# ScalarE's rounds in an experts' loop: eight pairs long in place of four, each pair's expert word loaded within the steps

## The chip, the cores and the metric

The kernel runs on one core of a Trainium2 chip. The metric is the device time of one execution, in microseconds (us); lower is better. Engines are named as the profile names them: PE is TensorE (PEld its weight loads), DVE is VectorE, ACT is ScalarE, POOL is GpSimd, SP is SyncE.

## The reference, cut to what matters

The input x has 4 batches of 1024 tokens of width 256. It is normalised, and the output is x plus an attention plus a mixture of experts, both of the normalised x. The part that the change touches is the mixture:

```python
def body(acc, ws):
    wg, wu, wdn, cw = ws
    hmid = jax.nn.silu(x @ wg) * (x @ wu)
    return (acc + cw[:, None] * (hmid @ wdn), None)
y, _ = jax.lax.scan(body, jnp.zeros_like(x), (We_gate, We_up, We_down, w_dense.T))
```

There are 64 experts of 256 x 128 (gate and up) and 128 x 256 (down), and every token picks 8 of them, so that the weight `cw` of most token and expert pairs is zero.

## The kernel before, in words

**The stages.** First the input is normalised, the router's scores are made and the slots of all token copies are worked out. Then attention is done for the first 18 of 32 blocks of 128 tokens, while GpSimd scatters copies of the tokens into a table in HBM in which each tile of 128 rows belongs to one expert. Then comes the experts' loop, and then the attention of the last 14 blocks, beside which the experts' results are added up. In the profiled execution the experts' loop fills about us 616 to 1218 of the span.

**The experts' loop.** There are 320 tiles, taken two at a time: 160 pairs (`PAIRS`). The tiles of a pair may belong to different experts. No scheduler is at work: each engine has its own instruction stream, written out by hand, and the streams meet at semaphores. For pair u they do this:

- ScalarE's queue loads the pair's rows, four pairs ahead (`load_pair`, L1265), into one of four buffers (`XS` = 4, shown as pr and qz).
- TensorE turns the pair's tiles into PSUM (`turn_tiles`, L966, 4 transposes), two pairs ahead; ScalarE copies them back (`keep_tiles`, L1243, sm<-psT).
- ScalarE copies the gate and up weights of the pair's two experts out of a ring of eight experts (`keep_weights`, L1261, two copies wt<-shared_mem), two pairs ahead, into one of two buffers. It has to know which experts: one word for each pair, e1 * 64 + e0, lies in `pair_row`, and `experts_of` (L1253) loads it into a register and takes the two numbers out of it.
- TensorE multiplies by gate and up (`gate_up`, L982, shown as 16 matmuls), one pair ahead; ScalarE applies Silu (`silu`, L1249, prT<-psS), VectorE multiplies the halves (`make_h`, L1683), TensorE multiplies by down (`down`, L991, shown as 4 matmuls), VectorE copies the result (`keep_y`, L1690), and GpSimd scatters it to HBM (L669).

TensorE's order in the step of pair u is `turn_tiles(u+2)`, `down(u-1)`, `gate_up(u+1)`. It may start `down(u)` when `make_h(u)` is done, and `gate_up(u+2)` when the weights and the turned tiles of pair u+2 are there. ScalarE's order in the step of pair u is `silu(u)`, `keep_tiles(u+2)`, `keep_weights(u+2)`, `load_pair(u+4)`.

**The rounds.** The loops are hardware loops over rounds of unrolled steps. TensorE's rounds are eight pairs long (`PE_ROUND`), and it loads each pair's word in the step before. VectorE's and GpSimd's are four long. ScalarE's are four long as well: 1 unrolled round of four, 38 in a hardware loop (L1288), 1 unrolled at the end, and at the head of each it loads the words of all four pairs whose weights it will copy. VectorE's rounds 1 to 32 hold extra work (`slot_weights`, L1494) for each pair.

Of the kernel before, what the change touches and what calls it, by code (L numbers as in the profile page):

```python
# [38 lines left out]
PAIRS = TILES // 2  # L39
MID_TILE = TILES // 2  # L40
assert MID_TILE <= 256
PE_ROUND = 8
XS, YS = 4, 4
ROW = 272
META = K + 1
# [12 lines left out]
MANY = 9  # L58
# [12 lines left out]
def build(nc, A, out):  # L71
    with ExitStack() as ctx:
# [6 lines left out]
        def sem(name):  # L79
            return ctx.enter_context(nc.semaphore(name))  # L80
# [254 lines left out]
        row_meta = sem("row_meta")  # L335
# [347 lines left out]
        def _(pe):  # L683
# [276 lines left out]
            def turn_tiles(j, u, turn, first):  # L960
                pe.wait_ge(xs_in[j], 16 * (turn + 1))
                if not first:
                    pe.wait_ge(xsT_ready, u - 1)
                for a in range(2):
                    for c in range(DC):
                        last = nc.tensor.transpose(psT[:, j % 2, (a * DC + c) * P:(a * DC + c + 1) * P],  # L966
                                                   xs[j][:, a, c * P:(c + 1) * P], ident[:])
                last.then_inc(xs_turned, 1)

            def experts_of(u):  # L970
                word = pe.value_load(pair_row[0:1, bass.ds(u, 1)], min_val=0, max_val=E * E - 1)
                return word % E, word // E
# [13 lines left out]
            def down(j, u, experts, first):  # L986
                pe.wait_ge(h_ready, u + 1)
                if not first:
                    pe.wait_ge(y_kept, u - 1)
                for a, e in enumerate(experts):  # L990
                    last = mm((psM, psO)[j % 2][:, a * D:(a + 1) * D], hT[:, j % 2, a, :], ring_d[:, e % RING, :],  # L991
                              start=True, stop=True)
                last.then_inc(pairs_done, 1)

            def round_of(g, first, final):
                u = g * PE_ROUND
                before = None if first else experts_of(u - 1)
                now = experts_of(u)
                for j in range(PE_ROUND):
                    if not (final and j >= PE_ROUND - 2):  # L1000
                        turn_tiles((j + 2) % XS, u + j + 2, g * (PE_ROUND // XS) + (j + 2) // XS, False)
                    if before:
                        down((j - 1) % XS, u + j - 1, before, first and j <= 2)
                    more = not (final and j == PE_ROUND - 1)
                    after = experts_of(u + j + 1) if more else None
                    if more:
                        gate_up((j + 1) % XS, u + j + 1, first and j == 0)
                    before, now = now, after
                return before

            def experts():
# [3 lines left out]
                round_of(0, True, False)  # L1015
                with pe.Fori(1, PAIRS // PE_ROUND - 1) as g:
                    round_of(g, False, False)
# [11 lines left out]
        def _(act):  # L1029
# [209 lines left out]
            def keep_tiles(j, u, first):  # L1239
                act.wait_ge(xs_turned, u + 1)  # L1240
                if not first:
                    act.wait_ge(gu_ready, u - 1)
                nc.scalar.copy(xsT[:, j % 2].rearrange("p a c t -> p (a c t)"), psT[:, j % 2, :]).then_inc(xsT_ready, 1)  # L1243

            def silu(j, u, first):
                act.wait_ge(gu_ready, u + 1)
                if not first:
                    act.wait_ge(h_ready, u - 1)
                nc.scalar.activation(sgT[:, j % 2, :, :], psS[:, j % 2, :].rearrange("p (a n) -> p a n", a=2)[:, :, 0:P],  # L1249
                                     ACT.Silu).then_inc(silu_ready, 1)  # L1250

            def experts_of(u):
                word = act.value_load(pair_row[0:1, bass.ds(u, 1)], min_val=0, max_val=E * E - 1)  # L1253
                return word % E, word // E

            def keep_weights(j, u, experts, first):
                if not first:
                    act.wait_ge(gu_ready, u - 1)
                for a, e in enumerate(experts):
                    act.wait_ge(experts_ready, e + 1)  # L1260
                    last = nc.scalar.copy(wt[j % 2][:, a, :, :], ring_gu[:, e % RING, :, :])  # L1261
                last.then_inc(wt_ready, 1)

            def load_pair(j, u):
                act.dma_start(xs[j], slot_pairs[u]).then_inc(xs_in[j], 16)  # L1265

            def step(j, g, nth, named, final=False):
                u = g * XS + j
                silu(j, u, nth < 2)
                if not (final and j >= XS - 2):  # L1270
                    keep_tiles((j + 2) % XS, u + 2, False)
                    keep_weights((j + 2) % XS, u + 2, named[j], False)
                if not final:
                    act.wait_ge(row_meta, u + 1)
                    load_pair(j, u + XS)

            def experts():
                act.wait_ge(experts_known, 16 * QT)
                for j in range(XS):
                    load_pair(j, j)  # L1280
                act.wait_ge(words_ready, 1)
                for j in range(2):
                    keep_weights(j, j, experts_of(j), True)
                    keep_tiles(j, j, True)
                named = [experts_of(j + 2) for j in range(XS)]
                for j in range(XS):
                    step(j, 0, j, named)
                with act.Fori(1, PAIRS // XS - 1) as g:  # L1288
                    named = [experts_of(g * XS + j + 2) for j in range(XS)]
                    for j in range(XS):  # L1290
                        step(j, g, MANY, named)
                named = [experts_of(PAIRS - XS + j + 2) for j in range(XS - 2)]
                for j in range(XS):
                    step(j, PAIRS // XS - 1, MANY, named, final=True)

            attention(0, FIRST)
            act.wait_ge(masked, 2 * FIRST * NPAIR)
# [2 lines left out]
            for j in range(2):  # L1300
                act.wait_ge(scattered[j], 16 * K * (NB // 2))
            experts()
            act.wait_ge(xs_turned, PAIRS)
            act.wait_ge(pairs_done, PAIRS + 1)
# [465 lines left out]
```

## Time and profile before

| what | value |
|---|---|
| median of 3 runs | 1569.08 us (1569.03 to 1569.74) |
| the profiled execution's own time | 1555.25 us |
| its span in the profile | 1553.5 us |
| busy share of the span: PE, DVE, ACT, POOL | 86%, 60%, 55%, 40% |
| mean granted clock of TensorE | 0.925 |

The page gives shares of the whole span. The experts' loop is 39% of it, and the change touches that alone, so the views below are of windows in it. Two things are to be known of the trace: the ends of matmuls are modelled by the profiler, and an engine's register and branch instructions are not counted as busy: the time before an instruction in which nothing held it but such instructions is shown as "issue".

### The profile page before, as it was taken

To read this page: it belongs to the slowest core of one execution; us is meant where nothing else is said; L and a number is where in the kernel's file an instruction comes from. 1 tells how busy PE (TensorE), PEld (TensorE's weight loads), DVE (VectorE), ACT (ScalarE), POOL (GpSimd) and SP (SyncE) were. 2 spreads that over 40 slices of the span, in tenths; PEclk is the share of its full clock that TensorE was granted. 3 is DMA by queue.
4 is the path that set the end of the run, shared out by engine and by line. 5 is a ranking of instruction groups with operands and counts; after the bars stand their busy time and mean duration, and the time that the engine had idled before them with its cause. 6 is when DMAs were issued, how large, how long until landed. Compare 5 with 4: busy or idle time off the path is not lost.

```text
span 1553.5 us, 38499 instructions
## 1 busy us (share of the span) xinstructions
PE 1330.9 (86%) x9262; PEld 1181.9 (76%) x9263; DVE 933.4 (60%) x4527; ACT 850.4 (55%) x2382; POOL 626.7 (40%) x750
## 2 busy tenths in 40 slices
PE   5873878788787897988888898988899789999996
PEld 5863767677666786877777777777787789999995
DVE  6771434334334453666666565665644589888997
ACT  2442565565555585554545454454555467777774
POOL 7026555556555500555555555655555300000000
PEclk9986788788898797999999999999999989999998
DMA  7034443532222200566666666666544443333322
GB/s 243 32 126 147 143 160 125 171 132 94 92 93 86 86 7 30 175 186 187 193 189 195 182 185 189 190 186 187 168 151 143 171 153 96 117 109 103 122 91 75
DMA packets 152813, 214.06 MB, mean 138 GB/s; under 512 B 25268, under 2 KB 125365, under 8 KB 148149
## 3 DMA queue, kind: packets, MB, share of 16 engines
q1 hardware_dynamic: 80450, 86.77, 17.7%
q0 software_dynamic: 28800, 82.20, 14.1%
q10 hardware_dynamic: 43520, 44.57, 11.3%
q8 instruction: 19, 0.31, 0.1%
q14 instruction: 24, 0.20, 0.0%
HBM read 113.86 MB, written 103.81 MB: 140 GB/s over the span
## 4 chain that ended last, share of the span: by engine, by line
PE 60%; DVE 12%; issue 11%; ACT 6%; another core or an unknown queue 5%; ACTq 2%; SPq 1%; DVEq 1%; DMA 1%
PE psS L982 19%; PE psO L991 5%; PE psM L991 4%; DVE x_all L1656 4%; PE psT L862 4%; PE psT L966 3%; PE psS L847 3%; PE psV L819 3%; PE psV L790 2%; PE psS L832 2%; ACT pr L1147 2%; PE psQ L752 2%; PE psT L876 2%; PE psQ L800 1%
## 5 line engine op out<-in xcount | busy, mean ns | idle before, releaser
L982 PEld LDWEIGHTS psS<-sm,wt 128*128 128x128 f32 x2560 | 304.2, 192 | 56.1 <-issue 50.3
L982 PE MATMUL psS<-sm,wt 128*128 128x128 f32 x2560 | 320.8, 278 | 16.7 <-ACT wt L1261 7.4
L641 POOL DMA_INDIRECT slot_rows<-x_out_st,idx_st x256 | 247.8, 968 | 175.0 <-issue 58.4
L669 POOL DMA_INDIRECT home_rows<-qz,row_idx x160 | 154.6, 966 | 207.3 <-DVE qz L1690 177.5
L1147 ACT ACTIVATE pr<-sm,nmax 128x192 f32<-128x192 f32 x512 | 205.5, 451 | 51.5 <-DVE nmax L1585 49.9
L1249 ACT ACTIVATE prT<-psS 128x256 f32<-128x256 f32 x160 | 61.9, 387 | 286.2 <-PE psS L982 182.6
L669 POOL DMA_INDIRECT home_rows<-sm,row_idx x160 | 154.4, 965 | 141.9 <-DVE sm L1690 99.7
L1155 ACT COPY prT<-psT 128x384 f32<-128x384 f32 x256 | 122.1, 477 | 149.3 <-PE psT L862 83.9
L1683 DVE TENSOR_TENSOR prT<-psS,prT 128x256 f32<-128x256 f32 x160 | 67.7, 423 | 203.8 <-ACT prT L1249 165.9
L1261 ACT COPY wt<-shared_mem 128x512 f32 x320 | 184.4, 633 | 4.8 <-issue 4.8
L862 PE MATMUL psT<-ident,pr 128*128 128x128 f32 x768 | 142.0, 297 | 49.4 <-ACT prT L1155 43.8
L1585 DVE CUSTOM_DVE_ANT_0 sm<-psS,pr 128x192 f32<-128x192 f32 x512 | 157.4, 354 | 39.4 <-issue 35.6
L862 PEld LDWEIGHTS psT<-ident,pr 128*128 128x128 f32 x768 | 98.3, 155 | 72.3 <-issue 67.0
L1583 DVE MEMSET met<- 1x1 f32 x256 | 15.1, 59 | 184.1 <-PE psS L847 114.0
L1656 DVE SCALAR_TENSOR_TENSOR x_all<-shared_mem,w,x_all (+1 forms) x256 | 122.7, 481 | 2.2
L991 PE MATMUL psO<-shared_mem,prT 128*128 x320 | 85.4, 389 | 35.5 <-DVE prT L1683 35.5
L832 PE MATMUL psS<-kT,qz 128*128 128x192 f32 x448 | 99.3, 345 | 3.0 <-DVE qz L1438 1.9
L1243 ACT COPY sm<-psT 128x512 f32<-128x512 f32 x160 | 93.5, 584 | 14.3 <-PE psT L966 10.2
L991 PE MATMUL psM<-shared_mem,prT 128*128 x320 | 85.6, 390 | 10.5 <-issue 8.3
L991 PEld LDWEIGHTS psO<-shared_mem,prT 128*128 128x128 f32 x320 | 54.4, 190 | 47.2 <-issue 43.1
L752 PE MATMUL psQ<-xTs,wqk 128*128 128x128 f32 x512 | 79.8, 320 | 3.3 <-DVE rv L1423 2.7
L847 PE MATMUL psS<-kT,qz 32*128 32x192 f32 x576 | 73.4, 372 | 4.7 <-DVE shared_mem L1462 2.6
(290 smaller groups left out, 2725.6 us busy)
## 6 DMA issues: line engine op xcount, KB each, us to landing
shared_mem<-home_rows SPq DMA_DIRECT2D x32, 1024.0 KB, 5.1
pr<-slot_rows ACTq DMA_DIRECT2D x120, 272.0 KB
qz<-slot_rows ACTq DMA_DIRECT2D x40, 272.0 KB
slot_rows<-wt SPq DMA_DIRECT2D x32, 272.0 KB
shared_mem<-in_L_ffn_We_gate SPq DMA_DIRECT2D x64, 128.0 KB
shared_mem<-in_L_ffn_We_up SPq DMA_DIRECT2D x64, 128.0 KB
shared_mem<-in_L_ffn_We_down SPq DMA_DIRECT2D x64, 128.0 KB
x_all<-in_L_attn_x SPq DMA_DIRECT2D x4, 1024.0 KB, 9.6
```

The source lines that it names most:

```text
L641: pool.indirect_dma_start(slot_rows, bass.IndirectOffsetOnAxis(ap=idx_st[:, j, k:k + 1], axis=0), x_out_st[:, j % 2, :], None).then_inc(sc ...
L669: pool.indirect_dma_start(home_rows, bass.IndirectOffsetOnAxis(ap=row_idx[:, j, a:a + 1], axis=0), ys[j][:, a, :], None).then_inc(y_out[j] ...
L832: last = mm(psS[:, p % 2, u * WIN:(u + 1) * WIN], qz[:, c, u, heads, :].rearrange("p h t -> p (h t)"), kT[:, c, u * UQ:u * UQ + WIN], star ...
L847: last = mm(psS[:, m % 2, u * WIN:(u + 1) * WIN], qz[r, c, u, 0:2, :].rearrange("p h t -> p (h t)"), kT[r, c, u * UQ:u * UQ + WIN], start= ...
L862: last = nc.tensor.transpose(psT[:, 0, a * P:(a + 1) * P], flat[:, a * P:(a + 1) * P], ident[:])
L982: last = mm(psS[:, j % 2, (2 * a + n) * P:(2 * a + n + 1) * P], wt[j % 2][:, a, c, n * F:(n + 1) * F], xsT[:, j % 2, a, c, :], start=(c == ...
L991: last = mm((psM, psO)[j % 2][:, a * D:(a + 1) * D], hT[:, j % 2, a, :], ring_d[:, e % RING, :], start=True, stop=True)
L1147: nc.scalar.activation(pr[:, p % 4, par, :], sm[:, p % 4, par, :], ACT.Exp, bias=nmax[:, p % 4, par:par + 1], scale=-1.0).then_inc(probs, 1)
L1155: nc.scalar.copy(prT[:, p % 2].rearrange("p a t -> p (a t)"), psT[:, 0, 0:3 * P]).then_inc(prT_ready, 1)
L1261: last = nc.scalar.copy(wt[j % 2][:, a, :, :], ring_gu[:, e % RING, :, :])
L1585: v.tensor_tensor_reduce(sm[:, p % 4, u, :], psS[:, p % 2, u * WIN:(u + 1) * WIN], mask[:, u * WIN:(u + 1) * WIN], -1.0, -FLOOR, ALU.add, ...
L1656: ins = v.scalar_tensor_tensor(x_all[:, t, :], row, w8[:, t, k:k + 1], x_all[:, t, :], ALU.mult, ALU.add)
```

## The change

One constant (`ACT_ROUND` = 8) and ScalarE's part of the experts' loop. `step` becomes `round_of`, which walks through the steps of a round and holds one pair's experts at a time: those of pair base + 2 are loaded at the round's head, and each step but the last loads, after `load_pair`, the word that the next step needs. The unrolled rounds at both ends stay four pairs long; the loop between them has 19 rounds of eight in place of 38 of four. No other engine's stream changes.

```diff
+ACT_ROUND = 8
...
-            def step(j, g, nth, named, final=False):
-                u = g * XS + j
-                silu(j, u, nth < 2)
-                if not (final and j >= XS - 2):
-                    keep_tiles((j + 2) % XS, u + 2, False)
-                    keep_weights((j + 2) % XS, u + 2, named[j], False)
-                if not final:
-                    act.wait_ge(row_meta, u + 1)
-                    load_pair(j, u + XS)
+            def round_of(base, steps, first=False, final=False):
+                named = experts_of(base + 2)
+                for n in range(steps):
+                    u = base + n
+                    j = n % XS
+                    silu(j, u, first and n < 2)
+                    if not (final and n >= XS - 2):
+                        keep_tiles((j + 2) % XS, u + 2, False)
+                        keep_weights((j + 2) % XS, u + 2, named, False)
+                    if not final:
+                        act.wait_ge(row_meta, u + 1)
+                        load_pair(j, u + XS)
+                    if n < (steps - 3 if final else steps - 1):
+                        named = experts_of(u + 3)
...
-                named = [experts_of(j + 2) for j in range(XS)]
-                for j in range(XS):
-                    step(j, 0, j, named)
-                with act.Fori(1, PAIRS // XS - 1) as g:
-                    named = [experts_of(g * XS + j + 2) for j in range(XS)]
-                    for j in range(XS):
-                        step(j, g, MANY, named)
-                named = [experts_of(PAIRS - XS + j + 2) for j in range(XS - 2)]
-                for j in range(XS):
-                    step(j, PAIRS // XS - 1, MANY, named, final=True)
+                round_of(0, XS, first=True)
+                with act.Fori(0, (PAIRS - 2 * XS) // ACT_ROUND) as g:
+                    round_of(g * ACT_ROUND + XS, ACT_ROUND)
+                round_of(PAIRS - XS, XS, final=True)
```

ScalarE's stream at the head of a loop round, before. TENSOR_LOAD fetches a pair's word, ISA rows are register arithmetic and waits, prT<-psS is Silu.

```order
L1288 ISA
L1253 TENSOR_LOAD pair_row
L1253 ISA x3
L1253 TENSOR_LOAD pair_row
L1253 ISA x3
L1253 TENSOR_LOAD pair_row
L1253 ISA x3
L1253 TENSOR_LOAD pair_row
L1253 ISA x2
L1246 REGISTER_ALU
L1248 REGISTER_ALU
L1249 ACTIVATE prT<-psS 128x256
```

Four loads stand there between the branch and the first Silu of the round, and none between that and the round's end. Of the change, at the same place (line numbers are one higher from here on):

```order
L1292 ISA
L1254 TENSOR_LOAD pair_row
L1254 ISA x2
L1247 REGISTER_ALU
L1249 REGISTER_ALU
L1250 ACTIVATE prT<-psS 128x256
```

One load is left. The other seven of a round of eight stand in the steps, here from the last weight copy of one step to the Silu of the next:

```order
L1262 COPY wt1<-shared_mem 128x512
L1266 ISA
L1266 DMA pr<-slot_rows 128x2x272
L1254 ISA
L1254 TENSOR_LOAD pair_row
L1254 ISA x2
L1250 ACTIVATE prT<-psS 128x256
```

Each now stands behind the issue of its step's row load and ahead of the next step's Silu.

## Rows read from the trace of the kernel before

**Rows 1.** The page: busy time by engine.

```profile
PE 1330.9 (86%) x9262; PEld 1181.9 (76%) x9263; DVE 933.4 (60%) x4527; ACT 850.4 (55%) x2382; POOL 626.7 (40%) x750
```

**Rows 2.** Busy time by stretch: us, each engine's busy time, clock, DMA share, GB/s.

```profile
622.00:634.00 12.00, 12.00 (x97) 11.69 (x97) 6.37 (x35) 8.04 (x16) 4.41 (x5) 0.99 0.45 126
680.00:1100.00 420.00, 375.73 (x2657) 326.53 (x2656) 267.33 (x1439) 207.87 (x444) 234.93 (x250) 1.00 0.63 189
1130.00:1216.00 86.00, 77.19 (x560) 68.28 (x559) 41.06 (x216) 45.57 (x96) 45.17 (x48) 1.00 0.47 142
```

**Rows 3.** Chain of waits, us 722 to 738: start, length, what.

```profile
722.40 0.44 DVE prT L1683
...
724.26 2.02 PE psS L982 x16
...
726.72 0.35 issue
727.07 1.13 PE psM L991 x4
...
728.26 2.02 PE psS L982 x16
...
737.61 0.44 DVE prT L1683
```

**Rows 4.** Chain of waits, us 624 to 634, the loop's first pairs.

```profile
627.50 0.44 PE psT L966 x4
627.93 0.87 PE psO L991 x4
628.80 1.78 PE psS L982 x16
630.58 0.44 PE psT L966 x4
```

**Rows 5.** Timeline of ScalarE, us 715 to 727; in brackets the idle time before.

```profile
721.99 0.38 ACT L1249 ACTIVATE prT<-psS 128x256 f32<-128x256 f32 x1 [4.15 <-PE psS L982]
...
722.73 1.15 ACT L1261 COPY wt<-shared_mem 128x512 f32 x2
726.00 0.38 ACT L1249 ACTIVATE prT<-psS 128x256 f32<-128x256 f32 x1 [2.12 <-issue]
...
727.79 0.40 ACT L1249 ACTIVATE prT<-psS 128x256 f32<-128x256 f32 x1
```

**Rows 6.** Timeline of TensorE, us 715 to 724.

```profile
716.22 1.95 PE L982 MATMUL psS<-sm,wt 128*128 128x128 f32 x16
...
721.09 0.60 PE L966 MATMUL psT<-ident,pr 128*128 128x128 f32 x4
723.05 1.12 PE L991 MATMUL psO<-shared_mem,prT 128*128 x4 [1.36 <-DVE prT L1683]
```

**Rows 7.** Who waited for whom, us 640 to 1100: us in total, times, longest.

```profile
ACT prT L1249 <- PE psS L982: 165.0, 60, 5.6
...
ACT prT L1249 <- issue: 59.5, 28, 2.2
...
PE psO L991 <- DVE prT L1683: 29.8, 28, 1.4
...
PE psM L991 <- issue: 7.4, 27, 0.4
```

**Rows 8.** Chain of waits, us 1190 to 1198, after VectorE's extra work has ended.

```profile
1190.36 2.02 PE psS L982 x16
...
1197.71 2.02 PE psS L982 x16
```

**Rows 9.** Chain of waits, us 616 to 618: one pair's word loaded alone.

```profile
617.13 0.29 ACTq L1253
...
617.64 0.02 ACTq L1253
```

**Rows 10.** DMA queues, us 664 to 1120: packets, MB, share of 16 engines.

```profile
q8 instruction: 1, 0.02, 0.0%
```

## The prediction, made before the changed kernel ran

> **What bounds the kernel now.** I read the page first, for the engines' shares, and then windows of the experts' loop, because the change touches nothing else. PE is busy for 86% of the span and no other engine for more than 60% [rows 1]. In the experts' loop this holds more strongly: PE 375.73 us of 420, with the clock granted in full (1.00, so 2.4 GHz), and ACT, which the change edits, only 207.87 [rows 2]. So ACT's own time is worth nothing as such. It is worth what PE waits for.
>
> How long a pair takes when PE never waits is seen at the loop's start: the transposes of one pair begin at 627.50, those of the next at 630.58, which is 3.08 us, made of 0.43 to 0.44 for L966, 0.87 for L991 and 1.78 for L982 [rows 4]. In the steady state four pairs take 737.61 - 722.40 = 15.21 us, or 3.80 each [rows 3]. Four times 3.08 is 12.32; about 2.9 us of each four pairs are lost.
>
> The chain, with ACT's and PE's timelines beside it, shows two losses in each four pairs.
>
> The first I call **the dry wait**. PE ends its last transpose at 721.09 + 0.60 = 721.69 and starts L991 at 723.05, after 1.36 us of waiting for DVE's L1683 [rows 6]. That one waited for ACT's L1249 at 721.99, which ACT had been waiting to start for 4.15 us, on PE's L982 [rows 5]. The odd thing is that PE's group of 16 matmuls for that pair is shown as over at 716.22 + 1.95 = 718.17 [rows 6], 3.8 us earlier. ACT was idle and is let go only about when PE has run out of work, so the signal of a finished L982 seems to come late while PE goes on running. I don't know why. The pattern is there in 28 of the some 30 rounds of the window, 29.8 us in all for PE [rows 7]. Behind such a wait the next L991 takes 1.12 in place of 0.87, L982 starts 0.09 later and takes 2.02 in place of 1.78 [rows 3, 4, 6]. The dry wait costs 1.36 + 0.25 + 0.09 + 0.24 = 1.94 us.
>
> The second is **the head wait**. ACT's last weight copy of the round ends at 722.73 + 1.15 = 723.88, and the next L1249 starts at 726.00, 2.12 us later, with nothing but "issue" ahead of it [rows 5]: that is the branch and the four loads of the round's head. PE, which needs that pair's L1683, then waits 0.35 us, and again its L991 takes 1.13, L982 starts 0.06 late and takes 2.02 [rows 3]: 0.35 + 0.26 + 0.06 + 0.24 = 0.91 us. The two losses together are 2.85, and 12.32 + 2.85 = 15.17 against the 15.21 seen.
>
> **The change part by part.** It takes three of the four loads from each head, and every second branch. 2.12 us for four is 0.53 a load [rows 5], the same as a load alone, 617.13 to 617.66 [rows 9]. A head then costs about 0.5 to 0.7 us. In the chain ACT has slack for this: the Silu at 726.00 could start at about 724.5, its product would be there some 0.85 us later, and PE asks for it at 726.72 [rows 3, 5]. So the head wait should be gone at every head.
>
> It adds a load of 0.53 us to each step, behind the issue of the row load. That issue is made while the two weight copies (1.15 us) run [rows 5]. Issue and load together are about as long as the copies, so most of the load lies beside them. Between ends: 0, if ACT then waits for PE anyhow, as it did 60 times for 165.0 us [rows 7]; or 0.1 to 0.2 us for a step in which ACT is behind, as between 726.00 and 727.79 [rows 5]. That is in ACT's time. I take 0 for PE's. The row loads are issued in the same place as before, relative to the copies, so DMA, SP's queue, POOL and DVE get nothing new to do; only a faster PE would ask more of them, and at 3.08 a pair DVE, at 267.33 us of 420 [rows 2], would be at 78%.
>
> What is late next is the dry wait, and it decides the sum, since nothing in the change removes it. The question is after how many pairs it comes back once the head wait, which lets PE run dry as well, is gone. For n pairs from one dry wait to the next, a pair costs 3.08 + 1.94 / n. Now the two waits lie one pair apart, and from the head wait to the next dry wait it is three pairs.
> - If it stays tied to every fourth pair, n = 4: 3.57 a pair, 0.23 less.
> - If it comes three pairs after PE last ran dry, n = 3: 3.73, 0.07 less.
> - In the last part of the loop, where DVE's extra work is over, PE already ran in another cycle, two pairs in 1197.71 - 1190.36 = 7.35 us, 3.68 a pair [rows 8], in which the heads were covered. If the whole loop falls into that cycle: 0.12 less.
>
> The 3.80 holds from about us 640, where the windows of the waits begin [rows 7], to 1130, where those of the last part do [rows 2], so for 490 / 3.80 = 129 pairs. The three cases are worth 30, 9 and 15 us; the last part of the loop stays as it is. I take 12 us, between the last two, as the row that shows PE running without head waits is the 3.68, and the count of three pairs is what the main part itself shows. On the profiled execution's 1555.25 us that gives 1543; the median of the runs shown, 1569.08, lies 14 us above that execution, a difference that I can't trace to any row, and the same 12 us off it is 1557. (0.2% of it, 3 us, is about what a measurement of this kernel can tell from no change.)
>
> **The rivals.**
> - **PE never runs dry.** The first pairs of the loop went at 3.08 us [rows 4]. If it is the heads that start the late signals, all pairs go like that: 129 x 0.72 = 93 us, and some of the last part, so down to about 1470. Against it: the late signals also come in the last part, where no head is exposed.
> - **No difference.** The load in each step, and the branch, cost as much as the head gave, or the dry wait simply takes up what the head wait leaves: within 3 us. For it: ACT was idle for most of the time, so a shorter ACT path may only wait longer.
> - **Slower: PE runs dry every second pair.** The place is PE's L991 behind DVE's L1683, the mechanism is the late signal of L982, now without the second pause that gave it a fresh start. At n = 2 a pair costs 3.08 + 0.97 = 4.05, 0.25 more, or 32 us: 1601. It decides from 3.08 + 1.94 / n > 3.80, n below 2.7 pairs between dry waits. For it: two-pair cycles exist in the last part. Against it: there each pause is shorter, 7.35 - 2 x 3.08 = 1.19 us.
> - **Slower: the longer loop body has to be fetched in each round.** In 456 us of the loop one packet of instructions moved [rows 10], so the four-pair body stays where it is. The body becomes about twice as long. The longest pause of ACT in rows 5, 4.15 us, if it were added 19 times and PE absorbed 2 us of it, gives some 40 us more, 1610.
>
> The Trainium skill ("Runtime: NRT & Kernel Launch", Instruction fetch mechanics) says that an engine other than PE holds 512 instructions in two blocks of 256, and that a taken branch to a block no longer held stalls for a fetch. By it a body of under 150 instructions fits in both kernels, and the trace agrees for the shorter one; it would speak against this change only if a body that lies across two blocks were fetched anew each time.
>
> **How the numbers follow.** The forecast's cases (12 us less, 5 to 17) get 0.50, the dry wait at every fourth pair (30 less, about 1540) 0.14, PE never dry 0.10, no difference 0.10, dry every second pair 0.13, the fetch 0.03. Faster by over 0.2%: 0.50 + 0.14 + 0.10 = 0.74. Same: 0.10. Slower: 0.16. The forecast's own range is 1550 to 1565. To leave out no more than 2 in 10, I give up most of "never dry" at one end and the worst of the slower cases at the other, and reach from 1525, which is more than n = 4 with some pairs at full pace, to 1580, a third of the way to a dry wait at every second pair.
>
> **What would show it.** Right: no L1249 with 2.1 us of "issue" ahead of it; the entry of PE's L991 psM behind "issue" (7.4 us, 27 times) gone; the wait of L991 for L1683 still there, at other distances than four pairs; 3.65 to 3.75 us a pair between us 640 and 1130. Wrong: pairs at 3.1 us, with no dry wait (the heads had started it), or dry waits every second pair and over 3.8 us a pair, or packets of instructions in the loop, or a wait of PE for ACT's weight copies that are late by the added load.

## The result: 1.25% slower, with PE dry at most second pairs

The change makes the kernel slower: 1589.41 us (median of 4 runs, 1585.28 to 1589.82) against 1569.05 (4 runs beside them, 1566.76 to 1569.74), a ratio of 1.0125, 95% interval 1.0098 to 1.0152. The prediction was 1557 in a range of 1525 to 1580. In two later series of runs the same kernel took 1.0075 (1.0038 to 1.0113) and 1.0087 (1.0055 to 1.0118) of the kernel before.

| | before | after |
|---|---|---|
| time of the profiled execution | 1555.25 us | 1589.82 us |
| first Silu of the loop to the last | 598.0 us | 619.3 us |
| a pair, from the Silu of pair 8 to that of pair 128 | 3.805 us | 3.998 us |
| a pair, pairs 132 to 156 (VectorE's extra work over) | 3.64 us | 3.68 us |
| of those 120 pairs, Silus more than 5.5 us behind the one before | 30 | 47 |

Of the 34.6 us between the two profiled executions 21.3 lie in the loop; the rest lies before it (9.5 us) and behind it. The ratio of the runs gives 20 us as well. "A pair" below is always worked out as in the third row, from the starts of two Silus 120 pairs apart: here 657.59 and 1137.40.

The page and the window 680 to 1100 of the changed kernel, to be set against [rows 1, 2] (us, busy time of PE, PEld, DVE, ACT, POOL, granted clock, DMA share, GB/s):

```profile
PE 1337.5 (84%) x9261; PEld 1187.3 (75%) x9263; DVE 909.1 (57%) x4527; ACT 855.5 (54%) x2382; POOL 630.5 (40%) x750
```

```profile
680.00:1100.00 420.00, 358.25 (x2521) 311.69 (x2521) 233.76 (x1374) 201.30 (x423) 223.95 (x236) 1.00 0.58 179
```

PE is busy for 358.25 us of 420 where it was 375.73, at the same clock: it waits longer.

The packets of instructions in us 640 to 1240, over which nearly all of the 19 rounds of the new loop run:

```profile
q8 instruction: 4, 0.07, 0.1%
q14 instruction: 2, 0.02, 0.0%
```

That is six packets, where the kernel before moved seven in the same window (4 and 3). The longer body isn't fetched anew in each round.

Who waited for whom in the changed kernel, us 640 to 1100 (us in total, times, longest), to be set against [rows 7]:

```profile
ACT prT L1250 <- PE psS L983: 173.2, 45, 4.9
...
PE psO L992 <- DVE prT L1683: 46.6, 44, 1.4
...
ACT prT L1250 <- issue: 9.5, 22, 2.7
...
PE psS L983 <- ACT wt L1262: 7.3, 9, 1.1
```

The edit did what it says: ScalarE's 59.5 us of "issue" ahead of Silu [rows 7] are 9.5. But PE's wait for VectorE came 44 times in place of 28, with 46.6 us in place of 29.8. PE's wait for ScalarE's weight copies grew as well, to 7.3 us from 1.1 (once) in the kernel before; the section on the prediction comes back to it. The timelines show the cycle. TensorE of the changed kernel, us 815 to 834 (start, length, what, and in brackets the idle time before):

```profile
817.73 1.12 PE L992 MATMUL psO<-shared_mem,prT 128*128 x4 [1.15 <-DVE prT L1683]
818.97 2.02 PE L983 MATMUL psS<-sm,wt 128*128 128x128 f32 x16
820.83 0.60 PE L967 MATMUL psT<-ident,qz 128*128 128x128 f32 x4
821.26 1.03 PE L992 MATMUL psM<-shared_mem,prT 128*128 x4
822.13 1.95 PE L983 MATMUL psS<-sm,wt 128*128 128x128 f32 x16
823.91 0.60 PE L967 MATMUL psT<-ident,pr 128*128 128x128 f32 x4
825.76 1.13 PE L992 MATMUL psO<-shared_mem,prT 128*128 x4 [1.25 <-DVE prT L1683]
...
831.92 0.60 PE L967 MATMUL psT<-ident,pr 128*128 128x128 f32 x4
833.82 0.48 PE L992 MATMUL psO<-shared_mem,prT 128*128 x1 [1.30 <-DVE prT L1683]
```

ScalarE of the same stretch:

```profile
816.56 0.38 ACT L1250 ACTIVATE prT<-psS 128x256 f32<-128x256 f32 x1 [4.28 <-PE psS L983]
...
818.45 0.38 ACT L1250 ACTIVATE prT<-psS 128x256 f32<-128x256 f32 x1
...
824.69 0.38 ACT L1250 ACTIVATE prT<-psS 128x256 f32<-128x256 f32 x1 [4.34 <-PE psS L983]
...
826.65 0.38 ACT L1250 ACTIVATE prT<-psS 128x256 f32<-128x256 f32 x1
```

The L992 that had to wait start at 817.73, 825.76 and 833.82, two pairs and 8.03 and 8.06 us apart. The L983 of 818.97 is over at 820.99, and its Silu starts at 824.69, 3.70 us later, when PE has nothing left to run: the transposes of 823.91 are over at 824.51. The next Silu follows 1.96 us behind, without a wait. That is the dry wait of the prediction, here at every second pair; of the 47 late Silus of the table (over 5.5 us behind the one before), 36 come two pairs behind the late one before.

### The profile page after: what moved, and what is told of

It is laid out like the page before. It is cut to its first block, busy times and chain, and to the rows that moved or that the text cites. A ratio compares the mean times of both kernels' runs of the same rounds, so it can differ in the third digit from the quotient of the medians.

```text
span 1588.1 us, 38460 instructions
## 1 busy us (share of the span) xinstructions
PE 1337.5 (84%) x9261; PEld 1187.3 (75%) x9263; DVE 909.1 (57%) x4527; ACT 855.5 (54%) x2382; POOL 630.5 (40%) x750
## 4 chain that ended last, share of the span: by engine, by line
PE 54%; DVE 12%; another core or an unknown queue 12%; issue 9%; ACT 7%; ACTq 2%; SPq 2%; DVEq 1%; DMA 0%
PE psS L983 15%; PE psT L863 4%; DVE x_all L1656 4%; PE psO L992 4%; PE psM L992 3%; PE psS L848 3%; PE psV L820 3%; PE psS L833 2%; PE psV L791 2%; PE psT L967 2%; PE psQ L753 2%; ACT pr L1148 2%; ACT wt L1262 2%; PE psT L877 1%
## 5 line engine op out<-in xcount | busy, mean ns | idle before, releaser
L983 PEld LDWEIGHTS psS<-sm,wt 128*128 128x128 f32 x2560 | 303.6, 192 | 67.2 <-issue 62.3
L983 PE MATMUL psS<-sm,wt 128*128 128x128 f32 x2560 | 321.3, 279 | 25.9 <-ACT wt L1262 16.7
L992 PE MATMUL psO<-shared_mem,prT 128*128 x320 | 87.7, 396 | 50.7 <-DVE prT L1683 50.6
L992 PEld LDWEIGHTS psO<-shared_mem,prT 128*128 128x128 f32 x320 | 54.3, 189 | 67.8 <-issue 63.3
L992 PE MATMUL psM<-shared_mem,prT 128*128 x320 | 82.5, 380 | 2.6 <-DVE prT L1683 2.6
L833 PEld LDWEIGHTS psS<-kT,qz 128*128 128x128 f32 x448 | 73.4, 195 | 10.9 <-DVE qz L1438 6.8
```

The costliest lines, as they stand in the source:

```text
L833: last = mm(psS[:, p % 2, u * WIN:(u + 1) * WIN], qz[:, c, u, heads, :].rearrange("p h t -> p (h t)"), kT[:, c, u * UQ:u * UQ + WIN], star ...
L983: last = mm(psS[:, j % 2, (2 * a + n) * P:(2 * a + n + 1) * P], wt[j % 2][:, a, c, n * F:(n + 1) * F], xsT[:, j % 2, a, c, :], start=(c == ...
```

## The experiments

All are compared with the kernel before, run on the same chip between them. Unless it is said otherwise the diffs are against the changed kernel.

**Is it the length of the round, or the place of the loads?** The first experiment has rounds of four with the loads in the steps, the second rounds of eight with all eight loads at the head.

```diff
-ACT_ROUND = 8
+ACT_ROUND = 4
```

> The changed kernel with ScalarE's rounds four pairs long again (38 in the loop) and the loads still within the steps, one at each head. Pause theory (the old head kept ScalarE away for 2.1 us in every fourth pair, and that pause is what made TensorE run dry at every fourth pair and not at every second; round length as such does nothing): this kernel has no such pause either, so it runs like the changed one, 4.0 to 4.05 us a pair, 1583 to 1592 us. Length theory (the body of eight pairs is what costs): back to 1565 to 1572 us. Load theory (a load within each step stands in ScalarE's path): 1583 to 1592 us too; the next two runs part it from the pause theory.

```diff
-                named = experts_of(base + 2)
+                named = [experts_of(base + n + 2) for n in range(steps - 2 if final else steps)]
...
-                        keep_weights((j + 2) % XS, u + 2, named, False)
+                        keep_weights((j + 2) % XS, u + 2, named[n], False)
...
-                    if n < (steps - 3 if final else steps - 1):
-                        named = experts_of(u + 3)
```

> Rounds of eight, all eight words loaded at the round's head, none in the steps. Load theory: no load in a step, half as many branches: 1560 to 1569 us. Length theory: 1585 us or more. Pause theory: one pause of about 4.2 us in eight pairs, longer than TensorE can cover (it covers some 2.7 us), so about 1.5 us exposed in each of 19 rounds, and between the pauses the two-pair cycle of 8.05 us: 1580 to 1600 us.

Rounds of four with loads in the steps: 1588.91 us, ratio 1.0142 (1.0103 to 1.0181), 4.007 us a pair. That is the changed kernel again, so the length of the round doesn't matter. Rounds of eight with eight loads at the head: 1621.37, ratio 1.0329 (1.0288 to 1.0371), 4.218 a pair. That fits the length theory's open range, which the first experiment rules out, and lies above the 1580 to 1600 of the pause theory: the long pause cost PE some 3.0 us each (42.3 us in 14 waits for VectorE in the window) where 1.5 was expected. ScalarE of this one, us 815 to 840, Silu alone:

```profile
815.83 0.38 ACT L1250 ACTIVATE prT<-psS 128x256 f32<-128x256 f32 x1 [4.64 <-issue]
817.62 0.40 ACT L1250 ACTIVATE prT<-psS 128x256 f32<-128x256 f32 x1
821.28 0.39 ACT L1250 ACTIVATE prT<-psS 128x256 f32<-128x256 f32 x1 [1.75 <-PE psS L983]
827.25 0.39 ACT L1250 ACTIVATE prT<-psS 128x256 f32<-128x256 f32 x1 [3.90 <-remote]
829.03 0.40 ACT L1250 ACTIVATE prT<-psS 128x256 f32<-128x256 f32 x1
835.30 0.39 ACT L1250 ACTIVATE prT<-psS 128x256 f32<-128x256 f32 x1 [4.36 <-PE psS L983]
837.09 0.40 ACT L1250 ACTIVATE prT<-psS 128x256 f32<-128x256 f32 x1
```

There are no loads in its steps, and still the late Silus at every second pair are back (827.25, 835.30). So the loads in the steps aren't what slows the changed kernel. What is common to all three is that no pause of about 2 us comes every four pairs.

**Put the pause back and nothing else.** The words that the steps load stay; every fourth pair gets three more loads of the same word ahead of its Silu, which is work without use.

```diff
                     silu(j, u, first and n < 2)
...
+                    if j == 0 and not first:
+                        for _ in range(3):
+                            named = experts_of(u + 2)
```

> The changed kernel plus three more loads of the same word ahead of the Silu of every fourth pair (two such places in a round of eight), so that ScalarE stops for some 2.1 us there as it did before. Only work is added. Pause theory: TensorE runs dry at every fourth pair again, 3.8 to 3.85 us a pair, 1566 to 1575 us, faster than the changed kernel by some 18 us. Load theory and length theory: the added loads cost or change nothing, 1589 us or more.

1558.81 us (10 runs), ratio 0.9932 (0.991 to 0.9955), 3.790 a pair: faster than both kernels, by added work alone. The pause theory had said 1566 to 1575; the kernel did a little better. Waits of this kernel, us 640 to 1100:

```profile
ACT prT L1250 <- PE psS L983: 108.8, 51, 4.5
...
ACT prT L1250 <- issue: 54.6, 37, 3.1
...
PE psO L992 <- DVE prT L1686: 15.6, 20, 1.3
```

ScalarE's pauses are back (54.6 us, [rows 7] had 59.5), and the time for which PE waits for VectorE's product is down from 46.6 us to 15.6. Of the 120 Silus 29 are over 5.5 us behind the one before, where the changed kernel has 47. **The pause that the change removed held the dry waits apart.**

How it does that can be read in the kernel before. ScalarE, us 726 to 738, Silu alone:

```profile
731.17 0.38 ACT L1249 ACTIVATE prT<-psS 128x256 f32<-128x256 f32 x1 [1.47 <-PE psS L982]
...
737.20 0.38 ACT L1249 ACTIVATE prT<-psS 128x256 f32<-128x256 f32 x1 [4.13 <-PE psS L982]
```

The head's pause makes PE wait for 0.35 us at 726.72. The L982 behind it is over at 728.26 + 2.02 = 730.28 [rows 3], and its Silu starts at 731.17, only 0.89 us later. The signal of the pair after that is late by over 3 us again (737.20), and PE runs dry. In the changed kernel the first L983 behind a dry wait is already late by 3.70 us.

**Does something in PE's stream hold the signal?** PE loads no words in this one. Its down product takes another, fixed weight, so the experts' outputs are another computation's; the number and shape of the matmuls are the same.

```diff
-                word = pe.value_load(pair_row[0:1, bass.ds(u, 1)], min_val=0, max_val=E * E - 1)
-                return word % E, word // E
+                return 0, 1
...
-                    last = mm((psM, psO)[j % 2][:, a * D:(a + 1) * D], hT[:, j % 2, a, :], ring_d[:, e % RING, :],
+                    last = mm((psM, psO)[j % 2][:, a * D:(a + 1) * D], hT[:, j % 2, a, :], wsd[:],
```

> The changed kernel with TensorE loading no words: its down product takes the shared expert's down weights at a fixed place in place of the expert's own (that is what is left out; the sizes are the same). It asks whether TensorE's word loads hold back the signal that its matmuls are done. If they do: the Silu follows its matmuls within 0.1 to 1 us, few dry waits are left, 3.1 to 3.4 us a pair, 1480 to 1530 us. If they don't: as the changed kernel, 1580 to 1595 us.

1575.17, ratio 1.0028 (0.9997 to 1.0058), 3.926 a pair, between the two expectations. PE waited for VectorE 40 times for 42.8 us in the window, against 44 and 46.6. The late signals stay, so PE's own word loads are not their cause. But the kernel is 0.9% faster than the one with rounds of four beside it (1588.91 us, 1.0142), and 35 of the 120 Silus are late (over 5.5 us) in place of 43. What part of that belongs to the loads and what to the fixed weights, no run shows.

**When does the signal come?** Here PE itself waits for its signal of `gate_up(u)`, between `turn_tiles(u+2)` and `down(u-1)`, in each step. It has nothing else to issue meanwhile.

```diff
                         turn_tiles((j + 2) % XS, u + j + 2, g * (PE_ROUND // XS) + (j + 2) // XS, False)
+                    pe.wait_ge(gu_ready, u + j + 1)
```

> The changed kernel with one more wait: in every step PE itself waits for its own signal that gate_up is over (gu_ready), behind the turning transposes of the next pair and ahead of down. Theory A (the signal of a finished gate_up is held back while PE has more to run, and is given at once when PE has run empty): PE pauses 0.3 to 0.6 us in every pair and has no dry wait of 1.94 us in every second one, so 3.6 to 3.75 us a pair in the main part against 4.0, 1540 to 1560 us, faster than the changed kernel by 2 to 3%. Rival B (the signal is late by 3 to 4 us by itself, whatever PE does): each pair takes 3.08 us and the lateness, over 6 us, and the kernel over 1850 us. Rival C (the pause costs what it gives): 3.9 to 4.05 a pair, 1580 to 1600 us.

This series of runs met a surprise: the kernel before took 1305.59 us in it (13 runs, 1300.48 to 1319.96). The section on the hardware below comes back to it. In that condition the signals were on time anyway, and the added wait only cost: 1359.68, ratio 1.0438 (1.0406 to 1.047), 3.538 a pair. It says nothing of late signals. The same goes for the three others of that series.

> The same wait of PE for its own signal, in every second step only. Theory A: one pause of 0.3 to 0.6 us takes the place of each dry wait of 1.94 us, and the pair between comes with its signal late by up to 3 us, which PE bears nearly: 3.4 to 3.7 us a pair, 1510 to 1550 us, faster than with the wait in each step. Rival B: one lateness of 3 to 4 us in each two pairs, about 4.8 us a pair, over 1680 us. Rival C (PE runs dry in the pair between as well): 3.9 or more a pair, 1575 us or more.

1321.31, ratio 1.0141 (1.011 to 1.0171), 3.293 a pair.

> The changed kernel with one extra load of the same word (in place of three) ahead of the Silu of every fourth pair, about 0.5 us of ACT's time; with the step's own load a pause of about 1 us. Theory (a pause of ACT that makes PE run dry at every fourth pair spaces the dry waits): the pause is too short to make PE wait, since ACT has about 1.5 us to spare there, so nothing changes: 3.95 to 4.05 a pair, 1580 to 1595 us. Rival (any irregularity breaks the two-pair cycle, however short): under 3.85 a pair and about 1560 us, as with three.

1298.58, ratio 0.9946 (0.9913 to 0.9978), 3.140 a pair, and of the 120 pairs none is over 5.5 us behind the one before.

> Seven extra loads at every fourth pair, a pause of about 4.2 us of ACT, twice as long as that of the kernel before. Theory: PE pays for the longer pause in full, some 2 us more in each four pairs than with three extra loads, and gets back at most one dry wait of 1.94 us: 3.8 to 4.3 a pair, 1560 to 1630 us. If a long pause gives more pairs at 3.08 us behind it than a short one, it is at the lower end; if, as with eight loads at the head of a round of eight, dry waits come in every second pair between, at the upper.

1365.77, ratio 1.0489 (1.0457 to 1.0521), 3.577 a pair.

The four were therefore run again where the signals are late. In the next series the kernel before took 1555.42 us.

> The changed kernel as it is, for its time and trace beside the kernel before on the chip of this call. The chip of the first four experiments ran the kernel before in 1569 us with PE's signals late; that of the second four ran it in 1306 us, and a variant of the changed kernel with one extra load went at 3.14 us a pair there, PE never dry. Theory D (the late signals belong to the chip or its state, not to the kernel, and the dry waits and the loss by this change exist only with them): where the kernel before takes about 1569, this takes about 1589 and 4.0 us a pair, ratio 1.01 to 1.015; where before takes about 1306, this takes 1290 to 1303, 3.09 to 3.12 us a pair, a ratio of 0.988 to 0.998. Rival (the one extra load was what helped there): on a chip of the fast kind this has dry waits and over 3.3 us a pair.

1567.47, ratio 1.0075 (1.0038 to 1.0113), 3.934 a pair, a smaller loss than expected; 43 of 120 Silus over 5.5 us behind the one before.

> The kernel before, for its trace on the chip of this call. Theory D: where it takes about 1306, there is no dry wait, and what is left is a part of the head wait, at most 0.35 us in four pairs: 3.09 to 3.2 us a pair in the main part; where it takes about 1569, 3.8 us a pair as first shown. In both the ratio is 1.00 within 0.003.

1551.92, ratio 0.9966 (0.9926 to 1.0006), 3.804 a pair: a second trace of the kernel before gives the cycle of the first one, to 0.001 us.

> PE waits for its own signal of gate_up in every step, as in the run before of this kernel, which was on the fast chip and took 1359.68 us, 3.54 us a pair: there the signals are on time, so it could tell nothing of late ones. On a chip with late signals: Theory A (held back while PE has more to run, given at once when it has run empty): a pause of 0.3 to 0.6 us a pair, 3.5 to 3.75 us a pair, 1530 to 1560 us. Rival B (late by 3 to 4 us whatever PE does): over 6 us a pair, over 1850 us. On a fast chip: 1355 to 1365 again.

1537.37, ratio 0.986 (0.9804 to 0.9916), 3.687 a pair: theory A. TensorE of this kernel, us 800 to 808:

```profile
801.16 2.02 PE L983 MATMUL psS<-sm,wt 128*128 128x128 f32 x16
803.02 0.60 PE L967 MATMUL psT<-ident,pr 128*128 128x128 f32 x4
803.46 1.09 PE L992 MATMUL psO<-shared_mem,prT 128*128 x4
804.62 2.02 PE L983 MATMUL psS<-sm,wt 128*128 128x128 f32 x16
```

and ScalarE:

```profile
803.22 0.39 ACT L1251 ACTIVATE prT<-psS 128x256 f32<-128x256 f32 x1 [1.37 <-PE psS L983]
...
806.68 0.38 ACT L1251 ACTIVATE prT<-psS 128x256 f32<-128x256 f32 x1 [1.40 <-PE psS L983]
```

L983 ends at 801.16 + 2.02 = 803.18 and Silu starts at 803.22; the next at 806.64 and 806.68. The signal that was 3.7 us late is 0.04 us behind the modelled end, once PE has nothing to issue behind it. It comes even while the four transposes of 803.02 still run. A pair takes 3.46 us here (804.62 - 801.16) in place of 3.08, as L992 and L983 have the longer forms that they have behind a pause (1.09 and 2.02), and only 6 of 120 Silus come over 5.5 us behind the one before.

> The same wait in every second step; on the fast chip it took 1321.31 us, 3.29 us a pair, so one such wait costs 0.4 us there. On a chip with late signals: Theory A: 3.3 to 3.6 us a pair, 1500 to 1545 us, faster than the changed kernel by 3% or more. Rival B: over 4.8 us a pair, over 1680 us. Rival C (PE runs dry in the pair between as well): 3.9 or more a pair, 1575 us or more.

1569.31, ratio 1.0086 (1.0052 to 1.0119), 3.976 a pair: rival C by the pace, though 6 us less in all than it said. TensorE of this kernel, us 800 to 812:

```profile
801.93 1.13 PE L992 MATMUL psO<-shared_mem,prT 128*128 x4 [1.19 <-DVE prT L1685]
...
809.84 1.13 PE L992 MATMUL psO<-shared_mem,prT 128*128 x4 [1.13 <-PE psS L983]
```

The wait for its own signal (31 times for 32.2 us in the window) stands just where the dry wait was. The signal of the pair between was late already, so the product that this `down` needs came no sooner.

**With the late signals held off, what is the change worth?** The same wait in the kernel before, to be set against 0.986.

```diff
                         turn_tiles((j + 2) % XS, u + j + 2, g * (PE_ROUND // XS) + (j + 2) // XS, False)
+                    pe.wait_ge(gu_ready, u + j + 1)
```

> The kernel before (rounds of four, loads at the head), with PE's wait for its own signal of gate_up in every step. With late signals the changed kernel with this wait took 0.986 of before, 3.69 us a pair; with signals on time 1.0438, 3.54. Theory (apart from the late signals the change does what was predicted of it, it takes the head wait away): this one keeps a head wait of 0.3 to 0.9 us in each four pairs, so it is 0.08 to 0.25 us a pair slower than the changed kernel with the same wait: ratio to before 0.992 to 1.008 with late signals, 1.05 to 1.07 with signals on time. Rival (the change is harmful by itself): its ratio is below 0.984, or below 1.04 with signals on time.

1529.96, ratio 0.9862 (0.9821 to 0.9902), 3.668 a pair. Neither of the two. The changed kernel with this wait had 0.986 (0.9804 to 0.9916) and 3.687 a pair, so within these intervals the change is worth nothing there. ScalarE of this kernel, us 800 to 815, Silu alone:

```profile
804.28 0.38 ACT L1250 ACTIVATE prT<-psS 128x256 f32<-128x256 f32 x1 [1.40 <-PE psS L982]
...
808.74 0.38 ACT L1250 ACTIVATE prT<-psS 128x256 f32<-128x256 f32 x1 [2.40 <-issue]
...
811.15 0.38 ACT L1250 ACTIVATE prT<-psS 128x256 f32<-128x256 f32 x1 [0.52 <-PE psS L982]
```

The head is there, with 2.40 us of "issue", and Silu comes 4.46 us after the one before; the next comes 2.41 us later. The two together are 6.87, two pairs of 3.44: PE has lost nothing. In the kernel before the Silu ahead of the head's was late as well (4.15 us of waiting ahead of it [rows 5]), and there the head did cost PE; with the late signals off, it has room. That last step is a reading of the two traces.

**How long must the pause be?** One extra load and seven, where three gave 0.9932.

```diff
+                    if j == 0 and not first:
+                        named = experts_of(u + 2)
```

> One extra load ahead of the Silu of every fourth pair, in the changed kernel. With signals on time it took 0.9946 of before. With late signals: if the pause must be long enough to make PE run dry (three extra loads, 2.1 us, gave 0.9932), about 1 us is too short, ratio 1.005 to 1.015 like the changed kernel, 3.9 to 4.05 us a pair; if any irregularity is enough, 0.99 to 1.00 and under 3.85.

1559.22 (10 runs), ratio 1.004 (1.0013 to 1.0067), 3.842 a pair, 29 Silus over 5.5 us apart. The ratio lies between the two expectations, the pace within the second: a pause of some 1 us breaks a part of the two-pair cycles.

```diff
+                    if j == 0 and not first:
+                        for _ in range(7):
+                            named = experts_of(u + 2)
```

> Seven extra loads at every fourth pair, a pause of 4.2 us. With signals on time 1.0489 of before, 3.58 us a pair, since PE pays for most of the pause. With late signals: the pause takes the place of one dry wait in four pairs and costs PE 2 to 2.5 us, so with at most one more dry wait 3.6 to 4.1 us a pair, ratio 0.97 to 1.03; if it makes PE's signals come in time in the pairs behind it, under 3.7.

1619.47, ratio 1.042 (1.0379 to 1.0461), 4.213 a pair, outside what was expected. With signals on time the same pause brought 30 Silus of 120 over 5.5 us apart, one for each pause; here there are 46, so in about half of the stretches between two pauses a dry wait comes on top of the pause.

> The changed kernel once more. With late signals 1.0075 to 1.0125 of before and 3.93 to 4.0 us a pair, dry every second pair. With signals on time (the kernel before about 1306 us): 3.09 to 3.12 us a pair, ratio 0.988 to 0.998, so faster.

1568.45 (6 runs), ratio 1.0087 (1.0055 to 1.0118), 3.938 a pair, where the kernel before took 1554.55: as expected of late signals. So the changed kernel itself was never seen with signals on time; what it is worth there is open. The variant with one extra load (0.9946) is the nearest.

With late signals, the extra loads in every fourth pair give this:

| extra loads | ratio to before | us a pair | Silus over 5.5 us apart, of 120 |
|---|---|---|---|
| none (the change) | 1.0087 | 3.938 | 41 |
| one | 1.004 | 3.842 | 29 |
| three | 0.9932 | 3.790 | 29 |
| seven | 1.042 | 4.213 | 46 |

In the last row 30 of the 46 are the pauses themselves. The row of three is from another series than the others, so it is the ratios that may be compared.

## Why the prediction was wrong

**The bound, right.** ScalarE's time is worth what PE waits for; ScalarE's pause fell by 50 us in the window of 640 to 1100, and PE's idle time there rose from 48 us to 66.

**The head wait, right in place and wrong in what it was worth.** The 2.12 us of "issue" are gone, as forecast. The prediction booked 0.91 us for each head. It did not book that the signal behind the head's pause comes nearly on time (0.89 us late in place of 3.70). In the kernel before, the dry waits come once in four pairs (30 of 120), so the pause kept about every second one away. By the prediction's own sums a dry wait costs 1.94 us, twice a head.

**The load in the steps, right as far as it shows.** 0 was taken for it. No run gives it by itself, but the kernel that keeps all of them and adds three more reached 3.790 us a pair, below the 3.805 of the kernel before, and the two-pair cycle came without them as well (eight loads at the head). One sign of being wrong that the prediction named did appear: PE waited for ScalarE's weight copies 9 times for 7.3 us (10 and 8 times in the later traces), in the kernel before once for 1.1. It isn't the load that made them late. ScalarE of the changed kernel, us 718 to 721:

```profile
719.84 0.58 ACT L1244 COPY sm<-psT 128x512 f32<-128x512 f32 x1 [1.09 <-remote]
720.32 0.62 ACT L1262 COPY wt<-shared_mem 128x512 f32 x1
```

The weight copies start late because the copy of the turned tiles ahead of them had waited for TensorE's transposes, and so it is at all nine places (0.37 to 1.12 us). It is a second form of the late signals.

**The step that failed** is the choice of n: "If it comes three pairs after PE last ran dry, n = 3". The prediction counted three pairs from the head wait to the next dry wait, where PE had waited only 0.35 us, and took that for the distance from one dry wait to the next. It isn't. At a dry wait two signals are given at once (Silus at 816.56 and 818.45), the signal of the next `gate_up` is held again, and PE is dry two pairs later: n = 2. The rival had exactly this mechanism, with 4.05 us a pair; the pure cycle of the changed kernel is 8.03 us in two pairs, 4.02, and the mean of the 120 pairs is 3.998 where the forecast had 3.65 to 3.75. It had a chance of 0.13 where the forecast had 0.50.

**The rival's size.** It priced 32 us, and 20 to 21 came. The pure cycle isn't everywhere: 3.998 a pair in the main part, 0.193 more than before, times 120 is 23 us, less 2 us that the first pairs gain. The cycle is broken now and then; in the second trace (3.934 a pair) more often, and the loss was 12 us.

**What spoke for the rival and was passed over.** [Rows 8] show pairs without an exposed head in a cycle of two, 7.35 us. The prediction read the 3.68 from it as a better rate and left aside that the distance was two. The reason given against it, that each pause there is shorter (1.19 us), holds for the last part alone: in the main part the same two pairs take 8.03. The wait in that last part is another one, too. One more line of the chain of [rows 8] shows it:

```profile
1197.01 0.57 ACT wt L1261
```

L982 starts at 1197.71, 0.13 us behind the end of this weight copy. So PE waits there for the weights and not for VectorE's product, and only the distance of two pairs carries over.

**The other rivals.** Never dry was wrong: the late signals don't need the heads. The fetch was wrong too: six packets of instructions moved in 600 us of the loop, no more than before, and eight pairs are 140 instructions of ScalarE in the trace. By the figures of the Trainium skill ("Runtime: NRT & Kernel Launch", Instruction fetch mechanics) both bodies fit, and the trace agrees for the longer one as well.

## What to carry to other kernels

Before you remove a wait, look at the one beside it: if two waits alternate, the shorter may be what spaces the longer, and taking it away makes the longer one come more often. Work out the cycle that remains from a stretch of the trace in which the removed wait is already absent, its period as well as its mean. And where a signal is late while its sender is busy, a wait of the sender for its own signal (1.4% gained here, in both kernels) is worth an experiment; where signals were on time, the changed kernel with it took 4.4% more than the kernel before.

## What the runs showed of the hardware

**PE's signals can be held back while it goes on.** The last matmul of a `gate_up` was over by its modelled end at 820.99, and ScalarE, idle, started at 824.69. The trace's semaphore events show the same: at 824.67 to 825.01 five signals of PE come within 0.34 us, two of `gate_up`, two of the transposes and one of `down`, 0.16 us after PE's last modelled end. When PE itself was made to wait for that signal, it took 0.04 us. The Trainium skill ("Perfetto Trace Analysis", Tensor Engine Instruction) says that the end of a matmul in a profile is estimated, and that the signal is sent when PSUM has acknowledged the writes. The first agrees with the profile's own account of its ends, but an error of the estimate can't be 3.7 us in one kernel and nothing in another, for the same 16 matmuls. The Trainium skill ("TensorE: Matmul & The Clock Gate", The cost: per-tile semaphore tail) gives 126 ns for the tail behind 16 tiles packed into the array with one increment; with late signals the late ones here are nearly 30 times that. What holds the signal is open: it is still late without PE's word loads and with either length of ScalarE's round, and a wait of PE ends it. What starts it is open as well. In the loop's first six pairs the changed kernel's signals were on time in two of its three traces.

**The same program, 260 us apart.** The changed kernel with one extra load took 1298.58 us in one series of runs and 1559.22 in another; the kernel before took 1305.59 in the first, and 1554 to 1569 in all others. Two of the series have the same chip number, 10, on record and lie some 16 minutes apart: one had its signals on time (1305.59), the next had them late (1555.42). If the number stands for one chip, the condition isn't a fixed property of it. Busy time in 300 us of the main part of the loop of the kernel with one extra load, first with signals on time:

```profile
520.00:820.00 300.00, 299.03 (x2289) 283.66 (x2288) 224.71 (x1237) 190.10 (x383) 202.90 (x216) 1.00 0.77 227
```

and with late signals:

```profile
700.00:1000.00 300.00, 262.30 (x1851) 229.35 (x1849) 170.75 (x997) 147.32 (x308) 163.37 (x173) 0.99 0.61 185
```

PE was busy for 299.03 us of 300, at 3.14 us a pair, and the clock was as good as fully granted in both. PE and ScalarE of the first, us 700 to 707:

```profile
700.46 1.95 PE L983 MATMUL psS<-sm,wt 128*128 128x128 f32 x16
...
703.54 1.95 PE L983 MATMUL psS<-sm,wt 128*128 128x128 f32 x16
```

```profile
702.44 0.39 ACT L1250 ACTIVATE prT<-psS 128x256 f32<-128x256 f32 x1 [1.03 <-PE psS L983]
...
705.53 0.38 ACT L1250 ACTIVATE prT<-psS 128x256 f32<-128x256 f32 x1 [1.03 <-PE psS L983]
```

700.46 + 1.95 = 702.41, and Silu starts at 702.44; PE never stops. Of the 252.7 us between the spans of the two profiled executions (1552.8 and 1300.1) 145.2 lie before the loop's first Silu (616.1 against 470.9), 106.3 from there to the last (603.7 against 497.4), and 1.2 behind. ScalarE's copies take the same time in both, 622 ns in the one and 629 in the changed kernel with late signals, and a matmul of L983 276 and 279 ns, so neither engine works more slowly. In the attention ahead of the loop the granted clock differs too, 1.00 against 0.84 in us 200 to 400 of this kernel and the changed one, which is 2.4 GHz throughout against a mix of that and 1.2 GHz. There PE was busy for 197.60 us of the 200 in the one and 161.21 in the other, so late signals may cost it the clock besides; whether they do, no run here tells. What puts a chip into the one condition or the other the runs don't show. It means that a tuning against late signals, as with the three extra loads, has been shown to help in one of the two conditions alone.
